# Two banks for the odd jobs of the first attention, two score banks for its exponentials, and other places for the combines of the last experts

## What is computed

```python
x = x + attn_a(layernorm(x))    # 16 heads of 8 channels, rotary positions, causal softmax, projection
x = x + ffn(layernorm(x))       # 64 experts, each token goes to the 4 with the largest sigmoid gates
x = x + attn_b(layernorm(x))    # one head, scores outside a band of 64 are 0 before the softmax
x = x + ffn(layernorm(x))       # the same experts again

# ffn: sel = sigmoid(x @ expert_sel.T); the top 4 per token; out = sum over the 4 of gate * relu(x @ keys[e]) @ values[e]
```

## Time and profile before

| | us |
|---|---|
| median of 3 runs | 1338.33 |
| lowest and highest | 1334.89, 1345.90 |
| the profiled execution | 1334.34 |
| its span, first to last instruction | 1332.4 |

### The profile page before, as it was taken

How to read it: one execution, slowest core, us unless ns; L and a number is a source line. 1 busy time by engine, 2 the same in 40 slices (tenths; PEclk the granted TensorE clock), 3 DMA queues, 4 the chain that set the end, 5 groups by cost and what they waited for, 6 DMA issues and landing times.

```text
span 1332.4 us, 20381 instructions
## 1 busy us (share of the span) xinstructions
PE 877.1 (66%) x6298; PEld 601.8 (45%) x6298; DVE 808.2 (61%) x2325; ACT 484.9 (36%) x1249; POOL 836.1 (63%) x1023
## 2 busy tenths in 40 slices
PE   1999988988899658798776453423288756964100
PEld 0334433333344227798675332313177756864100
DVE  2677888798887424664674874635586752653212
ACT  1156646565455513364443211101134323542000
POOL 5234647879766766287982647556367473996575
PEclk9999989999898858898897665555678887987655
DMA  6555533332261334587563101012125544863321
GB/s 191 200 193 198 190 125 119 97 94 95 70 213 54 90 104 118 153 243 223 165 168 91 45 28 51 35 37 84 31 72 163 153 143 121 239 182 114 100 68 53
DMA packets 206537, 163.67 MB, mean 123 GB/s; under 512 B 15968, under 2 KB 191072, under 8 KB 206432
## 3 DMA queue, kind: packets, MB, share of 16 engines
q1 hardware_dynamic: 185696, 112.00, 29.3%
q0 software_dynamic: 16384, 33.59, 7.9%
q10 hardware_dynamic: 4352, 16.78, 3.3%
HBM read 78.94 MB, written 83.36 MB: 122 GB/s over the span
## 4 chain that ended last, share of the span: by engine, by line
PE 34%; DVE 30%; POOL 14%; issue 11%; another core or an unknown queue 6%; DMA 2%; SPq 2%; ACT 1%; POOLq 0%; DVEq 0%; ACTq 0%
POOL v_aug L1621 8%; PE ps L697 6%; PE ps L706 5%; PE ps L600 5%; PE ps L538 4%; DVE x_res L1322 3%; PE ps L579 3%; PE ps L686 3%; PE ps L565 3%; DVE row_max L1096 2%; POOL w_attn L1604 2%; DVE st L1040 1%; DVE block_max L1096 1%; DVE dest_f L1291 1%
## 5 line engine op out<-in xcount | busy, mean ns | idle before, releaser
L1608 POOL DMA_INDIRECT sorted_rows<-xn,dest x256 | 253.2, 989 | 166.6 <-DVE dest L1295 107.2
L1621 POOL DMA_INDIRECT v_aug<-result_rows,dest x256 | 245.5, 959 | 132.1 <-issue 64.9
L883 ACT ACTIVATE arena<-ps 128x512 f32<-128x512 f32 x320 | 182.7, 605 | 105.9 <-PE ps L538 98.0
L697 PE MATMUL ps<-arena 128*128 128x128 f32 x1024 | 153.8, 299 | 54.8 <-DVE arena L1307 30.8
L565 PE MATMUL ps<-arena 64*128 64x128 bf16 (+3 forms) x576 | 142.8, 311 | 39.9 <-DMA arena<-k_parts 16.9
L872 ACT COPY arena<-ps 128x512 f32<-128x512 f32 x128 | 75.0, 586 | 254.3 <-PE ps L706 160.9
L697 PEld LDWEIGHTS ps<-arena 128*128 128x128 f32 x1024 | 140.1, 212 | 60.7 <-DVE arena L1307 32.9
L1307 DVE COPY arena<-ps 128x512 f32<-128x512 f32 x128 | 88.1, 689 | 125.6 <-PE ps L686 77.0
L706 PE MATMUL ps<-arena 128*128 x1024 | 148.2, 292 | 18.0 <-ACT arena L872 7.7
L1096 DVE TENSOR_REDUCE row_max<-ps 128x1 f32<-128x512 f32 (+1 forms) x192 | 128.9, 684 | 42.5 <-PE ps L579 39.8
L706 PEld LDWEIGHTS ps<-arena 128*128 128x128 f32 x1024 | 136.7, 208 | 20.0 <-issue 19.9
(11 more groups left out here) (190 smaller groups left out, 1302.9 us busy)
## 6 DMA issues: line engine op xcount, KB each, us to landing
arena<-sorted_rows SPq DMA_DIRECT2D x128, 256.0 KB
result_rows<-arena SPq DMA_DIRECT2D x128, 256.0 KB
sorted_rows<-arena ACTq DMA_DIRECT2D x16, 1024.0 KB, 4.4
arena<-q_parts SPq DMA_DIRECT2D x16, 512.0 KB
arena<-k_parts SPq DMA_DIRECT2D x16, 512.0 KB
q_parts<-parts SPq DMA_DIRECT2D x52, 128.0 KB, 2.8
k_parts<-parts SPq DMA_DIRECT2D x50, 128.0 KB, 2.9
sorted_rows<-xn,dest POOLq DMA_INDIRECT x256
```

Of the source, the lines that this page charges most:

```text
L697: mm = pe.matmul(ps[:, e_bank(2, layer, half, n), P * i:P * i + P], ktile[:, v, P * i:P * i + P], xtt[:, v, P * i:P * i + P], start=True, ...
L883: nc.scalar.activation(prob[:, grp % 2, pr % 2, PROB_AT[u]:PROB_AT[u] + T], ps[:, v % 3, :], ACT.Exp, scale=SCALE_A).then_inc(exp_done, 1)
L1608: g.indirect_dma_start(sorted_d[b // HALF][:, :], bass.IndirectOffsetOnAxis(dest[:, 16 * b + n:16 * b + n + 1], 0), xn1[:, b % 2, n // TOP ...
L1621: g.indirect_dma_start(yg[:, b % 2, i // TOPK, C * c:C * c + C], None, result_d[layer][b // HALF][:, :], bass.IndirectOffsetOnAxis(dest[:, ...
```

## The change

The odd jobs alternate between two banks, by their place in the table: those at even places write to bank 2, those at odd places to bank 7 (from iteration 8 on, all to bank 7). Each bank has its own pair of semaphores. Where a job needs what another one wrote and ACT or DVE took out, it now waits for that one by name (`NEEDS`). Bank 2 is taken from the exponentials' units, which now alternate between banks 0 and 1, so PE waits for the exponential of two units before. In the last half of the experts only two combines stand between the steps, behind steps 13 and 26; those of batches 2 to 6 follow behind the steps. The gathers of batch 2 are no longer paced. The combine of the last batch and its store are done in two halves, each when its eight gathers have landed.

```diff
-COMBINE_AT = (12, 19, 26, 33)
+COMBINE_AT = (13, 26)
...
+NEEDS = {"Q": "XT", "K": "XT", "V": "XT", "YT": "Y3", "PJ": "YT", "LG": "NT"}
...
 def job_numbers():
 
-    n, out = 0, {}
+    n, out = [0, 0], {}
     for it in range(FIRST_IT, LAST_IT + 1):
-        for _, _, name, off in JOBS:
+        for order, (_, _, name, off) in enumerate(JOBS):
             if there_is(name, it + off):
-                out[name, it + off] = n
-                n += 1
+                at = 1 if it >= B else order % 2
+                out[name, it + off] = at, n[at]
+                n[at] += 1
     return out
...
-        misc = ps[:, 7, :]
-        miscb = ps[0:32, 7, :].bitcast(BF16)
+        misc_banks = (ps[:, 2, :], ps[:, 7, :])
+        misc_bytes = (ps[0:32, 2, :].bitcast(BF16), ps[0:32, 7, :].bitcast(BF16))
...
-        misc_ready = sem("misc_ready")
-        misc_free = sem("misc_free")
+        misc_ready = [sem(f"misc_ready{i}") for i in range(2)]
+        misc_free = [sem(f"misc_free{i}") for i in range(2)]
...
+        def made(name, b):
+
+            at, n = job[name, b]
+            return misc_ready[at], n + 1
+
+        def emptied(name, b):
+
+            at, n = job[name, b]
+            return misc_free[at], n + 1
+
+        def misc_of(name, b):
+            return misc_banks[job[name, b][0]]
...
-            for b in range(B):
-                sp.wait_ge(combined, 16 * (B + b + 1))
-                sp.dma_start(out_d.rearrange("(t p) c -> p t c", p=P)[:, TT * b:TT * b + TT, :],
-                             x[:, TT * b:TT * b + TT, :]).then_inc(done_out, 16)
-            sp.wait_ge(done_out, 16 * B)
+            for half in range(2 * B):
+                if half % 2 or half >= 2 * B - 2:
+                    lo = TT * (half // 2) if half < 2 * B - 2 else 2 * half
+                    sp.wait_ge(combined, 16 * B + 8 * (half + 1))
+                    sp.dma_start(out_d.rearrange("(t p) c -> p t c", p=P)[:, lo:2 * half + 2, :], x[:, lo:2 * half + 2, :]).then_inc(done_out, 16)
+            sp.wait_ge(done_out, 16 * (B + 1))
...
             def begin(name, b):
-                n = job[name, b]
+                at, n = job[name, b]
                 if n:
-                    pe.wait_ge(misc_free, n)
+                    pe.wait_ge(misc_free[at], n)
...
                 v = 5 * pr + u
-                if v >= 3:
-                    pe.wait_ge(exp_done, v - 2)
+                if v >= 2:
+                    pe.wait_ge(exp_done, v - 1)
...
-                    return pe.matmul(ps[:, v % 3, at:at + n], kk[rows, s, pair, P * j:P * j + P], qs[rows, s, pair, P * j:T],
+                    return pe.matmul(ps[:, v % 2, at:at + n], kk[rows, s, pair, P * j:P * j + P], qs[rows, s, pair, P * j:T],
                                      start=True, stop=True)
...
             def run(name, b):
                 begin(name, b)
+                misc = misc_of(name, b)
+                if name in NEEDS:
+                    pe.wait_ge(*emptied(NEEDS[name], b))
...
+                        pe.wait_ge(misc_free[0], max(n for at, n in job.values() if at == 0) + 1)
...
                 if i or b:
-                    dve.wait_ge(misc_free, job[f"Y{i}", b])
+                    dve.wait_ge(*(emptied(f"Y{i - 1}", b) if i else emptied("Y3", b - 1)))
...
+            def combine_part(part):
+
+                b = B - 1
+                n = B + b
+                if part:
+                    dve.wait_ge(yg_last, 128)
+                else:
+                    dve.wait_ge(yg_in[b % 2], 256 * (n // 2) + 128)
+                for c in range(TOPK):
+                    dve.wait_ge(combined, 16 * n + 8 * part + 2 * c)
+                    for t in (2 * part, 2 * part + 1):
+                        xt = x[:, TT * b + t, :]
+                        nc.vector.scalar_tensor_tensor(out=xt, in0=yg[:, b % 2, t, C * c:C * c + C],
+                                                       scalar=top[:, TT * b + t, c:c + 1], in1=xt,
+                                                       op0=ALU.mult, op1=ALU.add).then_inc(combined, 1)
...
-            for b in range(HALF, B):
+            for b in range(len(COMBINE_AT), B - 1):
                 combine(1, b)
+            for part in range(2):
+                combine_part(part)
...
             for b in range(B):
-                gather(1, b, paced=b < HALF - 1)
+                gather(1, b, paced=b < 2)
```

More of the change, by code:

```diff
@@ L840, in take @@
             def take(name, b):
-                act.wait_ge(misc_ready, job[name, b] + 1)
+                act.wait_ge(*made(name, b))
+                return misc_of(name, b), emptied(name, b)[0]
             def fill(i):
@@ L1034, in take @@
             def take(name, b):
-                dve.wait_ge(misc_ready, job[name, b] + 1)
+                dve.wait_ge(*made(name, b))
+                return misc_of(name, b), emptied(name, b)[0]
             def ln_stats(src, st, mv, rs, b, seq, each=13, applied=None):
@@ L1357, in route @@
             def route(b):
-                yield from choose(b, misc_free, job["LG", b] + 1)
-                yield from chosen(b, misc_ready, job["RK", b - 1] + 1 if b else 0)
+                yield from choose(b, *emptied("LG", b))
+                yield from chosen(b, *(made("RK", b - 1) if b else (None, 0)))
             parts_work = route_work = place_work = owner_work = stats1_work = stats0_work = send_work = ()
@@ L1377, in _ @@
                     if at == (1, 4) and 0 <= last < B:
-                        place_work = positions(last, misc, misc_ready, job["RK", last] + 1, misc_free, job["RK", last] + 1)
+                        place_work = positions(last, misc_of("RK", last), *made("RK", last), *emptied("RK", last))
                         next(place_work)
@@ L1539, in _ @@
                     else:
-                        finish(chosen(B, misc_ready, len(job)))
+                        finish(chosen(B, *made("RK", B - 1)))
                 if prepare:
@@ L1646, in _ @@
                     if b:
-                        pool.wait_ge(misc_ready, job["XT", b - 1] + 1)
+                        pool.wait_ge(*made("XT", b - 1))
                     norm(b, mv0, rs0, rstd0, xn0, xn0_done)
@@ L1699, in _ @@
             g.memset(band, 1.0).then_inc(band_made, 1)
-            pool.wait_ge(misc_ready, job["Y3", B - 1] + 1)
+            pool.wait_ge(*made("Y3", B - 1))
             g.memset(probw[:, :, :, WIN + 1:], 0.0).then_inc(band_made, 1)
```

79 lines of the change are left out of this document (43 added, 36 removed).

## The result

Over 20 executions each, the changed kernel took 1346.34 us (median, 1339.11 to 1351.29) and the kernel before 1337.11 us (1331.97 to 1345.90). The ratio is 1.0058, 95% interval 1.0042 to 1.0074: slower by 0.58%, 7.8 us. I had forecast no change, 1336.5. Every ratio in this document leaves out the few executions that ran clearly slower than the rest of their kernel (1576 to 1972 us in e9, e12 and e15, for example). The profiled execution has a span of 1343.2 us, 10.8 more than before.

A forecast was written before the change was run, and what follows sets the result against it. No engine was taken as full: DVE, PE, ACT and POOL bind in turn, POOL's gathers at the end. Terms summed to -0.1 us, 1334.2; with +2.3 for a fresh median, 1336.5 us, no change, range 1318 to 1350.

The forecast's parts named there:

- the price of the two score banks, +4.0: First attention: units wait for the exponential two before; ten bursts at 0.4 us each, +4.0 us, bounds 0 and +16.
- PE idles for as long as before, only elsewhere, so I don't count on it: First attention: possible faster clock once odd-job waits go, left in the range only, at most -1.6 us a batch, -8 in all.
- Odd jobs in two banks, -1.5 and -3.7: First attention: PE's waits move to maxima units, -1.5 us over five batches; last batch's Y2 starts earlier, -3.7 us.
- The last half's steps, +3.4: Last expert steps: waits for gathers go, but unpaced gathers hold up steps; gather 4 starts +3.4 us later, bounds -23 and +12.
- The last batch halved, -2.3: Kernel's end: half the last combine runs beside the last eight gathers, -2.3 us, bounds -3 and 0.
- The sum: Whole kernel: -1.5 - 3.7 + 4.0 + 3.4 - 2.3 = -0.1 us, 1334.2 on the profiled execution's scale.
- the exponentials become the bound: First attention, rival: 32 copies of the values' bank delay exponentials and DVE idles; 19 us for 4, 1351.5, chance 0.08.

The follow-up runs named there:

- e9: Kernel before with combines behind steps 13 and 26 and the last batch halved, batch 2's gathers still paced: 0.9942 of before's 1225.8 us.
- e12: e1 with three unread matmuls filling PE's 0.37 us wait ahead of the third unit of slot 6 in each batch: 1.0036 of before's 1346.7 us.
- e15: Kernel before with only the tail's edits (two combines between steps, batch 2's gathers unpaced, last batch halved): 0.9996 of before's 1346.7 us.
- e1: Kernel before with only the exponentials' units cut from three score banks to two, odd jobs left in one bank: 1.0127 of before's 1225.5 us.
- e2: Changed kernel with the tail of before put back, so only the first attention's edits remain: 1.0051 of before's 1225.5 us.
- e4: Kernel before with only the last batch's combine and store done in two halves: 0.9971 of before's 1225.5 us.
- e13: e12 plus unread matmuls ahead of Y0, Y1 and the first maxima unit of slot 5, four waits filled: 0.9944 of before's 1346.7 us.
- e6: Kernel before with a memset behind every indirect transfer of second attention and expert layers, except the last four batches' gathers: 0.9716 of before's 1338.7 us.
- e11: Kernel before paced as in e6 (gathers up to batch 3), with combines behind steps 13 and 26 and the last batch halved: 1.0514 of before's 1225.8 us.

## Why the prediction was wrong

**The step that failed is the price of the two score banks, +4.0.** Its waits were right: ten bursts of 0.4 us were predicted, and nine waits of 3.4 us together stood there up to 410. But the term measured 15.6 us (e1), because it was priced by the waits alone and TensorE's clock behind them was left out. e12 puts what goes with the filled waits at about 11 of the 15.6, across two kinds of chips; 6.8 of it is seen in the four periods, with the granted clock at 0.88 against 0.92. The profile of before had the sign: the clock stood at 0.76 in one window, and the same eight value products took 1.94 us against 1.07. I wrote that "PE idles for as long as before, only elsewhere, so I don't count on it", and used it for the gain of the odd jobs only. A new gap of 0.4 us was not worth 0.4 us here. e12 is the measure: with that gap filled, the two banks cost 0.36%, 4.9 us, nearly the term.

**Odd jobs in two banks, -1.5 and -3.7.** Their sum was 5.2, measured 9.3 (e1 against e2, each known to about 3 us). The waits moved to the maxima units as said. In the last batch Y2 does wait for Y0's evacuation only, 459.17 against 458.82, but Y0 itself came 14.6 us late, with 11.5 at the batch's mark: 3 of the 3.7 us were lost ahead of it. Whether more of the gain lies in the steady batches than I took stays open: the four periods' 220.1 to 225.0 us in the four profiles with the odd jobs in two banks spread too widely against the 224.5 and 224.6 without.

**The last half's steps, +3.4.** Right in kind, 2.5 us too high: gather 4 moved by 12.8 - 11.9 = 0.9 us, and the steps beside the runs did stand for 8 to 16 us. Right for this kind of chip only. The Trainium skill, page "SBUF — State Buffer", section "Who interferes with whom", says that "PE and ACT never wait on anyone". On the chips at 1225 the traces agree (no "remote" wait of ACT from 600 to 1230), on those at 1337 to 1347 ACT does stand (170.0 us in before); what it waits for there the profile doesn't name.

**The last batch halved, -2.3.** 2.0 us in the changed kernel's profile, 3.6 in e4.

**The sum.** 15.6 - 9.3 + (0.9996 - 1) x 1346.7 = +5.8 us, and the change measured +7.8. The sum came near zero in the forecast by small terms, and near +6 here because two terms that were both too small have opposite signs and partly cancel. The rival "the exponentials become the bound" had nearly the size of the failed term (19), but not its cause: e12's exponentials are the same.

## What to carry to other kernels

Where PE is nearly full, price a new wait not by its length alone but by what the granted clock does in the period behind it, and look for that in windows of 5 us: here the fall came 14 us behind the new wait. A filler matmul into a free bank in such waits is cheap to try, and with four waits filled it beat the third score bank here (0.9944 in e13). Price the parts of a change in separate kernels: here one lost 15.6 us, one gave back 9.3 and one was worth 15 us or nothing. What happens beside back-to-back indirect transfers has to be measured on more than one chip before a schedule is built on it.

## What was not expected of the hardware

The same program took 1225 us on some chips and 1337 to 1347 on others, with the first attention alike to 1 us over four batches. The difference grows almost wholly beside back-to-back indirect transfers, where ACT has 170.0 us of waits in the one and none in the other, single ones of 33.8 us. Pacing them gained 2.84% on the one kind (e6), and with the new tail lost 5.1% on the other (e11).

With a new wait of 0.37 us once a batch the mean granted clock over 220 us was 0.88, and 0.92 with that wait filled; the difference was 7 us there. The Trainium skill, page "Perfetto Trace Analysis", section "Matmul Optimizations", says that the matrix engine scales its power with its use, so that matmuls should stand back to back; e12 and e13 agree, with 6.8 and 14.8 us in four batches.
